# An eight-core attention and FFN kernel: first two head pairs projected and bounded by 512 tokens, attention entered at the last transposed tile

## The reference

```python
x = L0_attn_x                                  # (8, 2048, 1024)
xn = _layernorm(x, axis=-1)
s = _L0_attn_ref(xn, Wq, Wk, Wv, Wo)           # 16 heads of 64, RoPE on q and k, causal softmax, out projection
g = _silu(_L0_ffn_ref(xn, ...))                # LayerNorm again, dequantized fc1 (1024x4096), silu, fc2, residual + 0.5 z
return x + s * g
...
scores = jnp.einsum('bhqd,bhkd->bhqk', q, k) / dk ** 0.5
scores = jnp.where(causal, scores, -jnp.inf)
attn = jax.nn.softmax(scores, axis=-1)
out = jnp.einsum('bhqk,bhkd->bhqd', attn, v)
```

## Time and profile before

| | |
|---|---|
| median of 3 runs | 1046.03 us (1046.02 to 1047.77) |
| the profiled execution's own time | 1046.82 us |
| its span, slowest core (7) | 1045.3 us; cores 1028.5 to 1045.3 us |
| TensorE busy | 940.6 us (90%) |
| VectorE, ScalarE, POOL busy | 425.9 (41%), 492.6 (47%), 78.5 us (8%) |
| mean granted clock of TensorE, core 7 | 0.979 |

### The profile page before, as it was taken

How to read it: one execution, slowest core, us unless ns; L and a number is a source line. 1 busy time by engine, 2 the same in 40 slices (tenths; PEclk the granted TensorE clock), 3 DMA queues, 4 the chain that set the end, 5 groups by cost and what they waited for, 6 DMA issues and landing times.

```text
span 1045.3 us, 17142 instructions; the slowest of 8 cores (1028.5 to 1045.3 us)
## 1 busy us (share of the span) xinstructions
PE 940.6 (90%) x6430; PEld 439.1 (42%) x6430; DVE 425.9 (41%) x709; ACT 492.6 (47%) x637; POOL 78.5 (8%) x162
## 2 busy tenths in 40 slices
PE   1678788899899989998789999999999999999997
PEld 0455333444454434543234444444444444444443
DVE  3475455656564646565551111000014333333333
ACT  4753566778787868877784333334410000000000
POOL 1332110101010101022000000000000000000000
PEclk9999989999999999999899999999999999999999
DMA  9764875566566666553128999765294143413111
GB/s 226 198 139 119 162 192 172 170 195 188 176 203 196 183 195 183 205 178 127 66 83 238 297 304 288 200 145 138 87 315 150 55 151 132 149 60 143 61 60 41
DMA packets 89632, 171.74 MB, mean 164 GB/s; under 512 B 8416, under 2 KB 45424, under 8 KB 88432
## 3 DMA queue, kind: packets, MB, share of 16 engines
q1 hardware_dynamic: 76768, 152.23, 46.0%
q0 software_dynamic: 12784, 18.43, 9.8%
HBM read 132.41 MB, written 37.76 MB: 163 GB/s over the span
## 4 chain that ended last, share of the span: by engine, by line
PE 74%; ACT 9%; issue 6%; DVE 5%; DMA 4%; POOL 0%; SPq 0%; DVEq 0%; ACTq 0%; POOLq 0%
PE ps L1091 21%; PE ps L1150 21%; PE ps L904 9%; PE ps L352 6%; ACT pb L875 5%; PE ps L853 5%; PE ps L1121 5%; PE ps L396 4%; DMA swp<-raw 3%; DMA xbuf<-x 1%; PE ps L597 1%; DVE raw L363 1%; ACT linv L922 1%; ACT linv L924 1%; DVE pb L886 1%
## 5 line engine op out<-in xcount | busy, mean ns | idle before, releaser
L875 ACT ACTIVATE pb<-ps,negub 128x1024 bf16<-128x1024 f32 (+1 forms) x320 | 298.4, 981 | 96.8 <-PE ps L853 95.3
L1091 PE MATMUL ps<-xn,w1t 128*128 128x512 bf16 x1024 | 221.2, 379 | 0.0
L1091 PEld LDWEIGHTS ps<-xn,w1t 128*128 128x128 bf16 x1024 | 100.1, 98 | 120.7
L1102 ACT ACTIVATE yst<-ps,b 128x512 bf16<-128x512 f32 x128 | 87.8, 687 | 130.8 <-PE ps L1091 130.8
L1165 ACT ACTIVATE tf<-tf 128x512 f32<-128x512 f32 x32 | 20.1, 629 | 258.0 <-DVE tf L1161 258.0
L352 PE MATMUL ps<-xn,wqk 128*64 128x512 bf16 x896 | 124.1, 396 | 4.3 <-DVE nm L458 2.5
L853 PE MATMUL ps<-qk,qk 64*128 64x512 bf16 (+3 forms) x640 | 102.7, 362 | 24.4 <-ACT pb L875 21.9
L1150 PE MATMUL ps<-w2a,ybuf 128*128 128x512 bf16 x512 | 115.7, 379 | 0.0
L1150 PE MATMUL ps<-w2b,ybuf 128*128 128x512 bf16 x500 | 113.1, 379 | 0.0
L904 PE MATMUL ps<-pb,v_tm 128*64 128x512 bf16 (+3 forms) x640 | 92.6, 366 | 18.2 <-DVE pb L886 13.5
L904 PE MATMUL ps<-pb,ones 128*64 128x512 bf16 (+3 forms) x640 | 89.8, 359 | 0.0
(11 more groups left out here) (106 smaller groups left out, 677.9 us busy)
## 6 DMA issues: line engine op xcount, KB each, us to landing
dqi<-fc_q SPq DMA_DIRECT2D x64, 512.0 KB, 5.3
dqs<-fc_scales SPq DMA_DIRECT2D x64, 512.0 KB, 7.1
y_spill<-yst SPq DMA_DIRECT2D x32, 512.0 KB, 6.0
ybuf<-y_spill SPq DMA_DIRECT2D x7, 2048.0 KB, 9.5
w_deq<-dqo SPq DMA_DIRECT2D x48, 256.0 KB, 2.6
xbuf<-x SPq DMA_DIRECT2D x16, 512.0 KB, 6.4
w1t<-w_deq SPq DMA_DIRECT2D x32, 256.0 KB, 6.1
xt<-x SPq DMA_DIRECT2D x16, 512.0 KB, 4.4
```

The source lines that it names most:

```text
L875: tok = SC.tick(lambda e: e.activation(fap(p, [[512, 2], [1, n]], offset=off), fap(z, [[512, 2], [1, n]], offset=off), AF.Exp, bias=bias, ...
L1091: fn = (lambda k, fc, f, tg: lambda e: e.matmul(ring[k], w1t[f % 4][:, 128 * fc:128 * (fc + 1)], xn[:, S * fc + 512 * tg:S * fc + 512 * (t ...
L1102: t_ring[k] = SC.tick((lambda k, f, tg: lambda e: e.activation(yst[f % 3][:, 512 * tg:512 * (tg + 1)], ring[k], AF.Silu, bias=b1[:, f:f + ...
```

## The change

Pair 0's last quarter (`qk0(.., 3)`) and the last two V entries of the first two pairs leave the preamble and become the head of the filler. Pairs 0 and 1 are now treated as pair 7 was: exchange, squares, RoPE and bound by 512 tokens (`by_512`), with 4 bounds each. The bounds of pair 0's first two groups are made inside the preamble. `lead` falls from 24 to 8 entries. The filler of pairs 0 to 4 has more weight than that of pairs 5 to 7. Pair 3's RoPE comes 4 instead of 5 steps behind its exchange, pair 5's 4 instead of 3, pair 1's quarters 3.

```diff
@@ -363,12 +361,14 @@
                 t_raw[(m, j, tg)] = VE.tick(lambda e: e.tensor_copy(raw[j][:, 512 * tg:512 * (tg + 1)], p))
                 if bank is None:
                     f_free[state["b"]] = t_raw[(m, j, tg)]
-                if m == NP - 1:
-                    quarter7(j, tg)
+                if m in by_512:
+                    quarter(m, j, tg)
+                    if (j, tg) == (1, 3) and m + 2 < NP:
+                        t_wqk[m + 2] = load_wqk(m + 2, tok)
                 elif tg == 3:
                     swap(m, j)
                     square(m, j)
-                    later(3 if m in (1, 5) else 5, lambda: rope(m, j))
+                    later(4 if m in (3, 5) else 5, lambda: rope(m, j))
                     if j == 1 and m + 2 < NP:
                         t_wqk[m + 2] = load_wqk(m + 2, tok)
             return [(1.0, (lambda fc: lambda: one(fc))(fc)) for fc in range(NCH)]
...
+        by_512 = (0, 1, NP - 1)
+        t_s4, t_sq4, t_rope4, t_neg4, t_nm4, t_stb4 = {}, {}, {}, {}, {}, {}
+
+        def exchange(m, j, tg):
             lo, hi = 512 * tg, 512 * (tg + 1)
-            GP.wait(t_raw[(NP - 1, j, tg)], t_rope[(NP - 2, j)])
+            GP.wait(t_raw[(m, j, tg)], t_rope.get((m - 1, j)))
             for a, b in ((0, 32), (32, 0), (64, 96), (96, 64)):
-                t_s7[tg] = GP.dma(sl_s7[tg], swp[j][a:a + 32, lo:hi], raw[j][b:b + 32, lo:hi])
-            VE.wait(t_sqf[0], t_raw[(NP - 1, j, tg)])
-            t_sq7[(tg, j)] = VE.tick(lambda e: e.tensor_mul(
-                sq[:, 512 * j:512 * (j + 1)], raw[j][:, lo:hi], raw[j][:, lo:hi]))
+                t_s4[(m, tg)] = GP.dma(sl_s4[tg], swp[j][a:a + 32, lo:hi], raw[j][b:b + 32, lo:hi])
+
+        def square4(m, j, tg):
+            lo, hi = 512 * tg, 512 * (tg + 1)
+            at_sq = 1024 * (tg % 2) + 512 * j
+            VE.wait(t_sqf[0], t_raw[(m, j, tg)])
+            t_sq4[(m, tg, j)] = VE.tick(lambda e: e.tensor_mul(
+                sq[:, at_sq:at_sq + 512], raw[j][:, lo:hi], raw[j][:, lo:hi]))
+
+        def quarter(m, j, tg):
+            exchange(m, j, tg)
+            square4(m, j, tg)
             if j == 1:
-                later(3, lambda: products7(tg))
-
-        def products7(tg):
+                later(3, lambda: products(m, tg))
+
+        def products(m, tg):
             heavy[0] = True
             lo, hi = 512 * tg, 512 * (tg + 1)
-            VE.wait(t_s7[tg], t_last_s[NP - 3])
@@ -524,58 +531,63 @@
                     raw[j][:, lo:hi], raw[j][:, lo:hi], cos_t[:, lo:hi]))(j)))
             for j in range(2):
                 VE.wait(toks[j])
-                t_rope7[tg] = VE.tick((lambda j: lambda e: e.tensor_add(
-                    qb[(NP - 1) % 2][j][:, lo:hi], raw[j][:, lo:hi], swp[j][:, lo:hi]))(j))
-            t_rope[(NP - 1, 1)] = t_rope7[tg]
-
-        def norm7(tg):
-            b = side_bank()
-            PE.wait(t_sq7[(tg, 0)], t_sq7[(tg, 1)])
+                t_rope4[(m, tg)] = VE.tick((lambda j: lambda e: e.tensor_add(
+                    qb[m % 2][j][:, lo:hi], raw[j][:, lo:hi], swp[j][:, lo:hi]))(j))
+            t_rope[(m, 0)] = t_rope[(m, 1)] = t_rope4[(m, tg)]
+
+        def norm4(m, tg, z=None):
+            b = side_bank() if z is None else None
+            z = ps[3][:, 512 * b:512 * (b + 1)] if z is None else z
+            at_sq = 1024 * (tg % 2)
+            PE.wait(t_sq4[(m, tg, 0)], t_sq4[(m, tg, 1)], t_gp0)
             for j in range(2):
                 fn = (lambda j: lambda e: e.matmul(
-                    ps[3][32 * j:32 * (j + 1), 512 * b:512 * (b + 1)], hsel[:], sq[:, 512 * j:512 * (j + 1)],
+                    z[32 * j:32 * (j + 1), :], hsel[:], sq[:, at_sq + 512 * j:at_sq + 512 * (j + 1)],
                     start=True, stop=True, tile_position=(0, 32 * j), skip_group_check=True))(j)
                 if j == 0:
                     PE.do(fn)
                 else:
                     t_sqf[0] = PE.tick(fn)
             VE.wait(t_sqf[0])
-            t_nm7[tg] = VE.tick(lambda e: e.reduce_max(nm7[0:64, tg:tg + 1], ps[3][0:64, 512 * b:512 * (b + 1)],
-                                                       axis=AX.X))
-            f_free[b] = t_nm7[tg]
+            t_nm4[(m, tg)] = VE.tick(lambda e: e.reduce_max(nm4[0:64, 4 * m + tg:4 * m + tg + 1], z[0:64, :], axis=AX.X))
+            if b is not None:
+                f_free[b] = t_nm4[(m, tg)]
+
+        def rows4(m, tg, z=None):
+            b = side_bank() if z is None else None
+            PE.wait(t_nm4[(m, tg)], t_c)
+            tok = PE.tick(lambda e: e.transpose(z[0:1, 0:64], nm4[0:64, 4 * m + tg:4 * m + tg + 1], idn_f[0:64, 0:64]))
+            VE.wait(tok)
+            new = run4[0:1, 0:2] if tg == 0 else run4[0:1, 2:4]
             tok = VE.tick(lambda e: e.reduce_max(
-                new, ps[3][0:1, 512 * b:512 * b + 64].rearrange("p (a b) -> p a b", b=32), axis=AX.X))
-            f_free[b] = tok
+                new, z[0:1, 0:64].rearrange("p (a b) -> p a b", b=32), axis=AX.X))
+            if b is not None:
+                f_free[b] = tok
             VE.wait(tok)
...
+        def bc4(m, tg, z=None):
+            b = side_bank() if z is None else None
+            z = fb[b] if z is None else z
+            PE.wait(t_stb4[(m, tg)], t_gp0)
+            tok = PE.tick(lambda e: e.matmul(z[:, 0:1], ones_row[0:1, :], stb[0:1, 0:1], start=True, stop=True))
+            VE.wait(tok)
+            t_neg4[(m, tg)] = VE.tick(lambda e: e.tensor_copy(negub4[:, 4 * m + tg:4 * m + tg + 1], z[:, 0:1]))
+            if b is not None:
+                f_free[b] = t_neg4[(m, tg)]
...
-
-        t_rope0 = {}
-
-        def square0(tg):
-            lo, hi = 512 * tg, 512 * (tg + 1)
-                VE.wait(t_raw[(0, j, tg)])
...
-                    qb[0][j][:, lo:hi], raw[j][:, lo:hi], swp[j][:, lo:hi]))(j))
-            t_rope0[tg] = t_rope[(0, 1)]
+            exchange(0, j, tg)
...
-                if k == 3:
-                    later(3, (lambda tg: lambda: square0(tg))(tg))
-                    later(3 if tg > 0 else 5, (lambda tg: lambda: rope0(tg))(tg))
+                if k == 3 and tg < 2:
+                    later(3, (lambda tg: lambda: (square4(0, 0, tg), square4(0, 1, tg)))(tg))
+                    later(3 if tg > 0 else 5, (lambda tg: lambda: products(0, tg))(tg))
+
+                    later(4, (lambda tg: lambda: norm4(0, tg, ps[0][:, 512:1024]))(tg))
+                    later(5, (lambda tg: lambda: rows4(0, tg, ps[1][:, 512:1024]))(tg))
+                    later(6, (lambda tg: lambda: bc4(0, tg, ps[0][:, 512:1024]))(tg))
             step()
         while put_off:
             step()
         for j in range(2):
-            qk0(j, 3)
-        for k in range(2):
-            v0(6 + k, lambda out: later(1, out))
+            square4(0, j, 2)
         for b in range(2):
             f_free[b] = t_ev[NT - 2 + b]
         now[0] = 0
+        later(1, lambda: products(0, 2))
...
-        order = [("v", 1, range(0, 4)), ("q", 1, None), ("q", 2, None), ("v", 1, range(4, 6)),
-                 ("q", 3, None), ("v", 1, range(6, 8)), ("q", 4, None), ("v", 2, range(0, 6)),
+        order = [("t", 0, 3), ("t", 1, 0), ("t", 1, 1), ("v", 0, range(6, 8)), ("t", 1, 2), ("t", 1, 3),
+                 ("q", 2, None), ("v", 1, range(0, 6)), ("q", 3, None), ("v", 1, range(6, 8)), ("q", 4, None), ("v", 2, range(0, 6)),
                  ("q", 5, None), ("v", 2, range(6, 8)), ("q", 6, None),
-                 ("v", 3, range(0, 6)), ("t", 0, None), ("t", 1, None),
-                 ("v", 3, range(6, 8)), ("t", 2, None), ("t", 3, None)]
-        extra = [(0.0, (1.0, lambda: norm_mm(0, 0))), (4.0, (1.0, lambda: norm_mm(0, 1))),
-                 (9.0, (0.2, lambda: bound_rows(0))), (20.0, (0.1, lambda: bound_bc(0))),
-                 (44.0, (0.1, lambda: g2_row()))]
+                 ("v", 3, range(0, 6)), ("t", NP - 1, 0), ("t", NP - 1, 1),
+                 ("v", 3, range(6, 8)), ("t", NP - 1, 2), ("t", NP - 1, 3)]
+        extra = [(2.0, (0.5, lambda: norm4(0, 2))), (9.0, (0.1, lambda: rows4(0, 2))),
+                 (18.0, (0.1, lambda: bc4(0, 2))), (108.0, (0.1, lambda: g2_row()))]
         units = []
         at_pos = 0.0
-                extra.append((at_pos + 84, (0.1, (lambda m: lambda: bound_bc(m))(m))))
+                extra.append((at_pos + 90, (0.1, (lambda m: lambda: bound_bc(m))(m))))
                 for j in range(2):
                     for tg in range(4):
                         units += unit(m, j, tg)
                 at_pos += 64
             elif what == "t":
-                extra.append((at_pos + 22, (0.5, (lambda m: lambda: norm7(m))(m))))
-                extra.append((at_pos + 28, (0.1, (lambda m: lambda: rows7(m))(m))))
-                extra.append((at_pos + 40, (0.1, (lambda m: lambda: bc7(m))(m))))
+                extra.append((at_pos + 22, (0.5, (lambda m, tg: lambda: norm4(m, tg))(m, part))))
```

(26 more changed lines are left out.)

69 lines of the change are left out of this document (15 added, 54 removed).

## The result

The changed kernel takes 1063.04 us (median of 4 runs, 1058.95 to 1205.27), the kernel before beside it on the same chip 1046.9 us. The ratio is 1.0132, with a 95% interval of 1.0084 to 1.018. Medians here are over all runs of a kernel, ratios over those alone in which no die was disturbed, so a ratio can differ from the quotient of two medians. The profiled execution took 1058.95 us, its slowest core 1057.4. The prediction had said 1038.

A forecast was written before the change was run, and what follows sets the result against it. TensorE was taken to bound undisturbed pairs. First exponential 84.4, windows 441.8 and bounds 7.0 end attention at 533.2, 8.0 us before 541.2, so 1046.03 - 8.0 = 1038.0 us, own range 1032 to 1043.

The forecast's parts named there:

- The step that failed: Preamble: the first early bound delays the first exponential by 0 to 3.3 us, taken as 2.5.
- The rest of that sum: Start of attention: from 74.6 us, bound halves, squares, matmuls and score bring the first exponential to 84.4 instead of 91.91.
- the second bound's tail: Behind the preamble: the second early bound's two halves with nothing between, all idle, 3.3 us.
- The 12 matmuls of filler: Ahead of the first exponential: 12 matmuls, priced at 1.4 us.
- The sum of the windows: Attention on core 7: all pairs' windows and the end sum to 441.8 us, plus 7.0 for bounds.
- 7.0 for the bounds: Pairs 0 and 1: six bounds by group within attention at 1.2 us each, 7.0 us.
- The 0.24 us: Filler in every pair: each entry of 2 matmuls lengthens its window by 0.24 us; 48 moved entries make 11.5 us.
- Pairs 2 and 3 were to grow: Pairs 2 and 3: more filler entries lengthen their windows from 53.0 to 56.1 and from 53.8 to 57.2 us.
- Pair 4 came 1.2, pair 6 1.9 and the end 0.9 us longer: Later windows on core 7: pair 4 at 57.2, pair 6 at 53.1, the end unchanged at 29.9 us.
- The rival of the returning stop: Pair 1's quarter exchange waits behind a `wv` load, VectorE waits 3.6 us: 1041 to 1048, middle 1044; chance 0.2.
- as the prediction asked: Sign in the first pairs: granted clock above 0.95; a low clock anywhere there would be wrong.
- The bounds without cover: Pairs 0 and 1: six bounds cost 3.3 instead of 1.2 us each, 12.8 us on top, 1051; chance 0.1.

The follow-up runs named there:

- third experiment: The kernel before, plus two early bounds inside the preamble where the change makes them, results unused: 1070.74 us, ratio 1.027.
- eleventh experiment: The kernel before, plus two early bounds in the preamble, each VectorE reader one tile behind its TensorE half: 1052.86 us, ratio 1.0116.
- sixth: The changed kernel with early bounds' readers one tile later and step weight 1.3 instead of 1.2 for pairs 0 to 4: 1051.33 us, ratio 1.0075.
- tenth: The changed kernel with readers one tile later, pair 1 whole, lead 16, weights 1.23 for pair 0 and 1.1 for pairs 1 to 4: 1034.0 us, ratio 0.992.
- fourth experiment: The kernel before with only pair 1 made by quarters of 512 tokens, a bound for each: 1049.57 us, ratio 1.0065.
- seventh: The changed kernel with readers one tile later, pair 1 whole again, 16 entries of lead, weight 1.3 for pair 0: 1043.37 us, ratio 1.0002.
- first: The changed kernel with the bounds of pair 0's first two groups made behind the preamble, among the filler: 1053.49 us, ratio 1.0104.
- eighth: The changed kernel with readers one tile later, lead 16, filler between the second early bound's halves, group 2's bound moved too: 1051.82 us, ratio 1.0096.
- ninth experiment: The changed kernel with readers one tile later, weight 1.145 instead of 1.2 for pairs 0 to 4, keeping the filler list's end: 1039.9 us, ratio 0.9963.
- second: The changed kernel with each VectorE half of the two early bounds written one tile behind its TensorE half, in other banks: 1039.66 us, ratio 0.9958.
- the two partial moves: The changed kernel with only the first early-bound reader one tile later, 1046.29 us, ratio 1.0017; or only the second and third, 1058.4 us, ratio 1.0093.

## Where the prediction failed and where it held

**The step that failed** is the one on the first exponential: "The first bound lies inside the preamble, where VectorE and ScalarE hold each other up while the next tiles' statistics queue behind it: from 0 (all in other waits) to 3.3 (all exposed); I take 2.5". It named what is queued, and then bounded the price by the bound's own chain, 3.3 us from the earlier trace rows. But the chain in the earlier trace rows runs when no tile is left to normalise. In the preamble the wait of a reader lasts as long as what stands ahead of its matmul on TensorE, and that is a tile's transposes, which wait for ScalarE's norm, and its projections; what it holds up is the work that TensorE will need next. The last transposes came 20.2 us later and the first exponential 19.5 us after the forecast, against 2.5 us charged, and the third experiment shows it without the rest of the change. It also left out that the first reader of the second bound stands in the preamble too, 4.91 us of the 19.7.

**The rest of that sum holds within 1.5 us.** Without the 2.5 it gives 81.9, and with the readers moved the first exponential comes at 83.40. From the end of the last V product to the first filler pass 3.4 us (74.88 to 78.29) for the second bound's tail, 3.3 in the sum; in the eleventh experiment a bare tail took 4.08. The 12 matmuls of filler were mis-sized: 2.77 us instead of 1.4, in a stretch with a granted clock of 0.80.

**The sum of the windows** was right, 447.0 against 441.8 + 7.0 = 448.8, but by luck: its parts were off in both directions. Pairs 0 and 1 were priced at 56.4 and 56.7 with 7.0 for the bounds, 120.1, and take 120.0. But pairs 2 and 3, with nearly the same number of entries, take only 53.84 and 53.65. By that measure the first two pairs cost 12.5 us more than they would without what is particular to them, their bounds above all, and not 7.0. TensorE's waits for squares and readers in these two pairs, of the kind of the earlier trace rows, are 11.2 us in all, 1.9 for each of the six bounds and not 1.2:

```profile
PE ps L350 <- DVE negub L588: 3.8, 3, 1.4
...
PE ps L396 <- DVE run L563: 1.5, 1, 1.5
PE ps L560 <- DVE g2b L699: 1.4, 1, 1.4
PE ps L544 <- DVE sq L514: 1.3, 2, 1.0
```

An entry priced too high and a bound priced too low cancelled. Pairs 2 and 3 were to grow to 56.1 and 57.2 and take 53.84 and 53.65: TensorE's busy time in pair 2 grows from 49.16 to 51.47, 2.3 of the 3.1 us foreseen, and its idle time shrinks by 1.5 us, so that the pair grows by 0.8. The 0.24 us are about an entry's work, not its price while TensorE has idle time that it can fill. Pair 4 came 1.2, pair 6 1.9 and the end 0.9 us longer than foreseen. The sixth to tenth experiments show that such differences come from places, not from numbers.

**The rival of the returning stop** had a late exchange right and its effect wrong. The exchange whose DMAs are issued at 123.8 us, behind a `wv` load, lands 9 us later (last line: shortest, median and longest time to landing), the ones from 104 to 117 us in 2.0:

```profile
L60 POOL DMA_DIRECT2D swp<-raw x4: 496/496/513, 123.8 to 125.2; - x4
...
DMA to landing us min/median/max: 8.9/9.1/9.1
```

```profile
DMA to landing us min/median/max: 1.7/2.0/4.0
```

The rule of the Trainium skill that the prediction weighed ("DMA: Bandwidth & Descriptors", section "Two DMAs through the same engine are not ordered") agrees with these rows. They do not prove it: one of the four pieces issued just ahead of the load, from 120.1 us on, took 5.4 us too, two more 512 KB loads were issued on SyncE's queue at 121.64 and 122.11, and the late exchange of the fourth experiment stood ahead of its `wv` load. Order in the queue and sharing of the DMA engines are not told apart. The reader of the late exchange comes at 135.59 and waits 0.41 us; VectorE's longest wait for an exchange in pair 0 is 2.79 us, where it was 7.49. The clock is at 1.00 in pairs 0 and 1 as the prediction asked. In the fourth experiment, with other neighbours in the list, the stop is there, and in the sixth and seventh it is back in pair 6.

**The bounds without cover** were the slower rival, with 1051 and in pairs 0 and 1. The loss came by a related mechanism, a reader that waits with others queued behind it, but in the preamble, and there VectorE waited for TensorE and not for ScalarE. VectorE's waits for ScalarE in pair 0 became real in the first (2.32 us at 99.0 on core 7) and eighth experiments.

**What stays open.** The traces name the wait that makes pair 6 long in the kernels with another list, and pair 1 in the ninth experiment: TensorE stands for the copy or the maximum of a bound, which is queued on VectorE behind the RoPE products of a quarter. In pair 6 of the profiled executions this wait is 6.15 us (seventh, core 2), 5.20 (sixth, core 7) and 4.42 (second, core 2), and none over 1.9 us on cores 2 and 7 of the ninth and tenth; no run moved this reader alone. The 2.4 us more in fc1 on core 7 are for the most part a wait of TensorE for ScalarE's copy of `yst`, 2.3 us (`L1068`); ScalarE had waited itself, 10.4 us in three waits, for the stores `y_spill<-yst`. Single cores of other kernels lose more there, up to 515.8 us for fc1 and the rest (ninth, core 4, with 53.1 us of such waits), and it can decide which core is the slowest. Why these stores are late there was not sought. That the banks, which the moved readers also changed, have no part in the second experiment's gain was not tried alone; the two partial moves, which have the same banks, leave some 2 us for it if the effects add up.

## What to carry to other kernels

Where two engines hand work to each other tile after tile, an inserted pair of instructions can cost what stands ahead of its producer, not what it computes: before pricing it, read what is queued ahead of it on the producer's engine and what behind its reader on the other, and write the reader one stage later. Filler had no fixed price here: 13 entries more lengthened pair 2 by 0.8 us, and a shift of the list by a few entries cost more than the work moved, in part since a reader came to stand behind one that waits for a DMA. Two errors can hide in a sum that comes out right; compare the terms, not the sum. A change of a filler list should be judged by the length of every pair on every core, and its later places held fixed while its start is changed.

## Of the hardware, not expected

An exchange of 32 KB pieces issued 1.8 us behind a 512 KB load on the same queue landed in 9 us instead of 2, close to the end of the load, which landed in 11.9 us. In the preamble a tile's 32 V matmuls take 1.94 us at 56.26 and 2.85 at 64.31, behind an idle time of 4.86 us and in a stretch with a granted clock of 0.81: the stop is paid for again in the work behind it. In the eleventh experiment it is plainer: behind 4.08 us of standing still, 16 projections take 6.27 us at 0.56 instead of 3.63 us at 1.00.
